# Residual rows turned beside the norm and added on VectorE, in the place of two identity products

## The reference, cut to what matters

```
h = tok(x)                             # patches @ W + b, class token, positions
a = attn(h)                            # sigmoid paths, causal softmax per head, ctx @ Wo
x1 = h + a                             # the first residual: what the change is about
n = layernorm(x1)
f = layernorm(n) * gamma + beta
y = silu(f @ w1 + b1)                  # 256 -> 1024, dequantised weights
out = layernorm(n + 0.5 * (y @ w2 + b2))
```

## Time and profile before

| what | value |
|---|---|
| median of 3 runs | 178.4 us (176.03 to 178.91) |
| the profiled execution | 176.34 us |
| its span, first to last instruction | 174.6 us |
| PE busy | 154.1 us, 88% of the span |
| DVE busy | 94.3 us, 54% |
| POOL busy | 55.6 us, 32% |
| ACT busy | 48.0 us, 27% |
| granted TensorE clock | 0.999 of full |

### The profile page before, as it was taken

The page is one execution under the profiler, slowest core; times in us unless marked ns, Lnnn a source line. Parts: engine busy times, 40 slices in busy tenths (PEclk is TensorE's granted clock), DMA queues, the critical chain, the costliest instruction groups (busy, mean ns, idle before and its releaser), DMA issues.

```text
span 174.6 us, 2987 instructions
## 1 busy us (share of the span) xinstructions
PE 154.1 (88%) x1141; PEld 122.0 (70%) x1141; DVE 94.3 (54%) x175; ACT 48.0 (27%) x105; POOL 55.6 (32%) x129
## 2 busy tenths in 40 slices
PE   0289999799989999899999999999879969979980
PEld 0177878577667797487887778887658858868760
DVE  0065047557777956728647587647547443634232
ACT  0412112523243335114235324226022311032100
POOL 5009811032082603427107218106334022530011
PEclk9999999999999999999999999999999999999999
DMA  5999999700000000000100010000010000000000
GB/s 141 241 241 248 232 369 375 280 2 4 0 2 6 2 0 4 0 0 8 34 0 0 0 34 0 30 4 0 0 32 4 30 0 0 30 34 0 0 30 30
DMA packets 5501, 10.67 MB, mean 61 GB/s; under 512 B 715, under 2 KB 4400, under 8 KB 5232
## 3 DMA queue, kind: packets, MB, share of 16 engines
q1 hardware_dynamic: 5248, 10.30, 20.1%
q10 hardware_dynamic: 240, 0.19, 0.5%
HBM read 9.27 MB, written 1.21 MB: 60 GB/s over the span
## 4 chain that ended last, share of the span: by engine, by line
PE 83%; DVE 6%; DMA 4%; ACT 2%; POOL 2%; issue 1%; ACTq 1%; POOLq 0%
PE bank_z L555 20%; PE bank_s L542 18%; PE bank_z L436 7%; DMA vec_rows<-in_L_ffn_ln_beta 4%; PE bank_s L412 4%; PE bank_p L451 4%; PE bank_s L479 3%; PE bank_p L452 3%; PE bank_s L537 2%; PE bank_w L493 2%; PE bank_p L427 2%; PE bank_o L508 2%; PE bank_o L509 2%; PE bank_z L427 2%; PE bank_o L517 2%; PE bank_w L497 2%
## 5 line engine op out<-in xcount | busy, mean ns | idle before, releaser
L555 PE MATMUL bank_z<-w,act 128*128 128x256 f32 (+1 forms) x160 | 37.0, 381 | 1.8 <-DVE res L830 1.8
L542 PE MATMUL bank_s<-hnT,w 128*128 128x256 f32 (+1 forms) x160 | 35.2, 362 | 0.0
L555 PEld LDWEIGHTS bank_z<-w,act 128*128 128x128 f32 (+1 forms) x160 | 28.1, 182 | 8.0 <-issue 3.2
L542 PEld LDWEIGHTS bank_s<-hnT,w 128*128 128x128 f32 x160 | 28.9, 190 | 5.0
L821 DVE SCALAR_TENSOR_TENSOR act<-th,bank_s 128x512 f32<-128x512 f32 (+1 forms) x20 | 13.0, 648 | 20.3 <-ACT th L691 20.1
L337 POOL TENSOR_TENSOR rstd<-var,exponents 128x3 f32<-128x3 f32 (+1 forms) x10 | 8.9, 893 | 46.9 <-DVE var L805 46.9
L691 ACT ACTIVATE th<-bank_s 128x512 f32<-128x512 f32 (+1 forms) x20 | 11.3, 565 | 32.4 <-PE bank_s L542 32.4
L792 DVE RECIPROCAL recip<-bank_w 128x222 f32<-128x222 f32 (+1 forms) x11 | 16.4, 1494 | 0.7 <-PE bank_w L497 0.7
L675 ACT ACTIVATE phi_q<-bank_p 128x222 f32<-128x222 f32 (+1 forms) x11 | 3.9, 351 | 32.6 <-PE bank_p L461 32.6
L436 PE MATMUL bank_z<-xT,wT 128*128 128x288 f32 x48 | 12.6, 413 | 0.0
L787 DVE TENSOR_TENSOR probs<-probs,allowed 111x888 f32<-111x888 f32 (+1 forms) x11 | 11.5, 1046 | 1.9 <-ACT probs L685 1.9
(11 more groups left out here) (107 smaller groups left out, 242.0 us busy)
## 6 DMA issues: line engine op xcount, KB each, us to landing
x_rows<-in_x SPq DMA_DIRECT2D x6, 576.0 KB, 13.7
q<-in_L_ffn_fc_q SPq DMA_DIRECT2D x2, 1024.0 KB, 20.1
s<-in_L_ffn_fc_scales SPq DMA_DIRECT2D x2, 1024.0 KB, 22.1
out<-fin SPq DMA_DIRECT2D x9, 128.0 KB, 1.7
w_rows<-in_L_tok_W SPq DMA_DIRECT2D x3, 256.0 KB, 8.2
wvp<-in_L_attn_Wv SPq DMA_DIRECT2D x1, 256.0 KB, 10.2
wo<-in_L_attn_Wo SPq DMA_DIRECT2D x1, 256.0 KB, 17.1
b<-in_L_ffn_fc_bias ACTq DMA_DIRECT2D x1, 128.0 KB, 9.6
```

The lines of the kernel that those rows point to most:

```text
L542: last = mm(block[:, i], w1[:, e, f * 128:(f + 1) * 128], hnT[p % 2][:, e, 0:n], start=False, stop=(i == 1 and e == E2 - 1))
L555: last = mm(bank_z[0:w, 0:D], act2[:, f, in_pair(b)], w2[:, f, :], start=(f == 0), stop=(f == FB - 1))
```

## The change

The two identity products leave attention_out. In their place turn_residual(b) transposes the two halves of hT of block b into the second 256 columns of bank_o, residual_rows(b) copies these on ACT to h_rows in SBUF, and normalise(b) on DVE first adds h_rows and the product in bank_o into x1 (two buffers) and takes its statistics there; normed(b) reads x1 too. On PE turn_residual(b + 1) stands directly ahead of turn_normed(b) and waits for the same event, n2 of block b; turn_residual(0) stands in iteration 1, ahead of the patch product of that iteration. attention_out(b) now waits for the copied rows too.

```diff
@@ attention_out, PE
                 pe.wait_ge(ctxT_ready, done)
+                pe.wait_ge(hrow_ready, b + 1)
...
-                mm(bank_o[0:w, 0:D], ctxT[:, 1, tokens_of(b)], wo[:, 1, :], start=False, stop=False)
-                mm(bank_o[0:w, 0:128], hT[:, 0, tokens_of(b)], ident[:], start=False, stop=False)
-                mm(bank_o[0:w, 128:D], hT[:, 1, tokens_of(b)], ident[:], start=False, stop=True).then_inc(attn_psum, 1)
+                mm(bank_o[0:w, 0:D], ctxT[:, 1, tokens_of(b)], wo[:, 1, :], start=False, stop=True).then_inc(attn_psum, 1)
+
+            def turn_residual(b):
+                w = width(b)
+                if b > 0:
+                    pe.wait_ge(n2_ready, b)
+                for e in range(E2):
+                    last = pe.transpose(bank_o[0:w, D + e * 128:D + (e + 1) * 128], hT[:, e, tokens_of(b)], ident[:])
+                last.then_inc(hrow_psum, 1)
@@ the loop, PE
                 if a in TURN_AT:
+                    turn_residual(TURN_AT[a] + 1)
                     turn_normed(TURN_AT[a])
...
                 if a == 1:
+                    turn_residual(0)
                     pe.wait_ge(hT_ready, 2 * E2 + 1)
                     project(2, 1)
...
             weigh(TILES - 1)
+            turn_residual(OUTS - 1)
             turn_normed(OUTS - 2)
@@ ACT
+            def residual_rows(b):
+                w = width(b)
+                act.wait_ge(hrow_psum, b + 1)
+                if b > 0:
+                    act.wait_ge(x1_ready, b)
+                act.activation(h_rows[0:w, :], bank_o[0:w, D:2 * D], ACT.Copy).then_inc(hrow_ready, 1)
...
                 if a in TURN_AT:
                     normed_columns(TURN_AT[a])
+                    residual_rows(TURN_AT[a] + 1)
@@ DVE
             def normalise(b):
                 w = width(b)
                 dve.wait_ge(attn_psum, b + 1)
-                dve.bn_stats(stats[0:w, :], bank_o[0:w, 0:D]).then_inc(stats_ready, 1)
+                dve.wait_ge(hrow_ready, b + 1)
+                tt(x1[b % 2][0:w, :], h_rows[0:w, :], bank_o[0:w, 0:D], ALU.add).then_inc(x1_ready, 1)
+                dve.wait_ge(x1_ready, b + 1)
+                dve.bn_stats(stats[0:w, :], x1[b % 2][0:w, :]).then_inc(stats_ready, 1)
...
-                ts(n2[b % 2][0:w, :], bank_o[0:w, 0:D], mv[0:w, 0:1], rstd3[0:w, 1:2], ALU.subtract, ALU.mult).then_inc(n2_ready, 1)
+                ts(n2[b % 2][0:w, :], x1[b % 2][0:w, :], mv[0:w, 0:1], rstd3[0:w, 1:2], ALU.subtract, ALU.mult).then_inc(n2_ready, 1)
```

More of the change, by code:

```diff
@@ L150, in vit_block @@
         n2 = [sb(f"n2_{i}", [128, D]) for i in range(2)]
+        h_rows = sb("h_rows", [128, D])
+        x1 = [sb(f"x1_{i}", [128, D]) for i in range(2)]
         carry = [sb(f"carry{i}", [128, D]) for i in range(4)]
@@ L198, in vit_block @@
         recip_ready, ctxT_ready = sem("recip_ready"), sem("ctxT_ready")
+        hrow_psum, hrow_ready, x1_ready = sem("hrow_psum"), sem("hrow_ready"), sem("x1_ready")
         attn_psum, stats_ready, mv_ready, var3_ready = sem("attn_psum"), sem("stats_ready"), sem("mv_ready"), sem("var3_ready")
@@ L718, in _ @@
                     x_columns(C + 2)
+                if a == 1:
+                    residual_rows(0)
                 if a in TURN_AT:
                     normed_columns(TURN_AT[a])
+                    residual_rows(TURN_AT[a] + 1)
                 if a in HIDDEN_AT:
@@ L723, in _ @@
                         tanh_of(HIDDEN_AT[a], j)
-            for b in (OUTS - 2, OUTS - 1):
-                normed_columns(b)
+            normed_columns(OUTS - 2)
+            residual_rows(OUTS - 1)
+            normed_columns(OUTS - 1)
             for j in range(4):
```

## The result

The changed kernel takes 180.47 us (median of 4 runs, 180.32 to 181.04) against 177.48 us before (median of 4, 176.03 to 178.91). The ratio is 1.023, with a 95% interval from 1.0186 to 1.0273. The changed kernel is slower; whether by more than 2% the interval leaves open. The predicted time was 180.8 us, the predicted ratio 1.014; the interval lies above that.

The account below looks back on a forecast made before the run. The norm's DVE strand, on or near the path at nine of ten blocks, was taken as the bound, not PE. 9c + 10t - 2.9 gave +2.4 us, 1.4% more, 180.8 us on the median; range 177.4 to 183.0.

Parts of the forecast that it names:

- The strand of the norm: DVE and POOL work (statistics, power, norm) beside PE up to L517; on the path or 0.25 us off at nine blocks.
- c: Growth of the DVE strand per block: add 0.46 less 0.13 saved by the norm from SBUF, 0.33 us; counted at nine blocks.
- t: Pair of residual transposes on PE directly ahead of L517, behind the wait for n: 0.23 us, counted ten times.
- the cover of ACT's copy: PE's other work between L517 and the next product, 3.4 us at shortest, hiding ACT's copy, costed at nothing.
- PE's gain of 0.44: Two residual products (L510, L511) removed from PE ahead of each block's statistics: 0.44 us less per block.
- The second and third rivals: Second: norm gains nothing from SBUF, +3.6 us, chance 0.14. Third: residual pair costs 0.44 us, +4.5 us, chance 0.06.
- The first rival: PE is the bound and the longer DVE strand hides: -2.1 us, 176.3 us; chance 0.12.

Follow-up runs that it names:

- the one with the copy instead: Kernel before, both identity products kept, plus a DVE copy of the product from PSUM to x1, read by statistics and norm: 180.31 us, 1.0251 of before.
- the moved line: Half of block 6's second feed-forward product moved ahead of block 8's transposes: 175.01 us in before, 177.76 in changed, 175.46 in changed with wait for x1.

## Why the prediction was right, and where it was not

The strand of the norm, not PE, sets when the transposes start at eight of the nine blocks behind which a residual is turned: shown. There they start 0.05 to 0.06 us after the norm ends, as in block 2 (70.66 and 70.72) and block 3 (81.25 and 81.31). Block 5 is the exception: there the norm ends at 108.00 and PE comes last, at 108.35. Block by block, from the starts of the work behind the turned norm in the chain of both profiled executions, each less its first patch product:

| block | forecast, us | measured, us |
|---|---|---|
| 0 | +0.79 | +0.81 |
| 1 | +0.56 | +0.82 |
| 2 | +0.06 | -0.07 |
| 3 | 0.00 | +0.01 |
| 4 | +0.35 | +0.27 |
| 5 | +0.03 | +0.18 |
| 6 | +0.38 | +0.30 |
| 7 | +0.12 | +0.09 |
| 8 | +0.56 | +0.66, of it 0.15 by the clock |
| 9 | -0.44 | +1.04, of it 1.52 by the clock |
| sum | +2.4 | +4.1, without the clock +2.4 |

**The terms.** The norm from SBUF costs 0.412 us against the 0.410 taken over from L845; from add to statistics it is 0.44 to 0.46 (144.49 to 144.93) against 0.46; the second pair of transposes adds 0.22 to 0.24 against 0.23; PE has no wait for ACT's rows. c and t hold. One reading in the prediction was off: the row at 52.97 in the earlier trace rows that ends the cover of ACT's copy is DVE's; PE's next product (L508) starts at 52.77, so the shortest cover is 3.25 us and not 3.4. Nothing hung on it.

**Where single blocks were off.** In blocks 4, 6 and 8 I started the add when the silu's record ends; it starts 0.61 us after the silu's start (143.88 to 144.49), 0.08 us before that end. Independence from the silu does not explain it: before, the statistics did not depend on it either and started 0.68 us after its start (90.44 to 91.12). In block 5 I let PE's gain of 0.44 run on to the turned norm, but PE then reached turn_phi 0.20 us too early for phi: a wait that the chain before did not show, because PE came later. In block 1 DVE stood still for 0.32 us between mean and variance:

```profile
56.84 0.22 DVE L832 SCALAR_TENSOR_TENSOR var<-var_scale,mv,var_shift 128x3 f32<-128x3 f32 x1 [0.32 <-DVE mv L828]
```

This gap stands at the same instruction in all five profiles of kernels with the add, and not in the one with the copy instead. Its cause is open. That these errors cancel in the sum is luck.

**What failed.** The term that is missing is the clock. The prediction raised PE's wait at block 8 from 1.87 to 2.4 us ("where PE waited 1.87 us already: c + t") and costed everything behind it at the durations of the trace before. Those were durations at a clock of 1.00. In the changed kernel's trace the clock behind that wait fell to 0.50, for 1.67 us, and all four of its executions have a mean of 0.988 to 0.990. The Trainium skill ("TensorE: Matmul & The Clock Gate", section "HAM oscillation") tells of such a fall: a burst of products starts at half clock when PE has waited between bursts. The trace agrees (0.50 behind waits of 2.19, 2.52 and 2.55 us here), and the recorded clocks show too that the same kernel need not do so in every execution. So the fall is not a price of the change alone: before pays it in ten of 18 executions, and its profiled execution, on whose rows the prediction rests, was one that did not.

**Why the time came out close all the same.** This was luck. 180.8 us was built as a ratio of 1.014 on a median of 178.4, and that is a time of the executions of before whose clock fell (177.68 to 180.02 us); the others lie at 174.93 to 177.10. So the forecast most likely had the clock's price in its base without knowing it, though the clocks of those three executions are not on record. The ratio of 1.023 sets the changed kernel's four executions, all with a fallen clock, against about 176.4 us (180.47 / 1.023), a time of executions of before whose clock held. So it holds the strand and the clock, and the forecast's +1.4%, the strand alone, was short of it. Among executions with a fallen clock the change costs 180.47 - 178.49 = 2.0 us, or 1.1% (178.49 is the median of the ten of before, which ran beside the experiments and not beside the changed kernel), and that is near the forecast. The second and third rivals, the only ones beyond 2%, would have given such a time by another mechanism (a dear norm, dear transposes); both are refuted by the durations above. The first rival, PE as the bound, fell most clearly: PE has 20 instructions less and the end came later.

## What to carry to other kernels

An engine that is 88% busy is not the bound where it waits: compare, place by place, when the two strands that meet there arrive, and count an edit only with what it does to the later one. Where PE waits ahead of dense work, price that work at the lower clock too, and compare executions of equal granted clock before a difference is put down to the change; a few products that are due anyway, moved into the wait, shorten the wait and held the clock in all 18 executions of the moved line here. When an instruction stands behind a wait that it does not need (here the turned residual behind the norm), give it its own wait: that one line was worth 1.8 us at an equal clock, and 3.5 us of the changed kernel's 4.2 with the clock that then held.

## What the hardware showed unexpectedly

In the traces the granted clock fell to 0.50 behind waits of 2.19 to 2.55 us and stayed there for some 3.4 us (over 5 us in one trace) of dense products; behind 1.87 and 1.88 us it was 1.00 (before, and the residual turned inside the wait). No length of wait that decides is shown: ten of 18 executions of before have the low mean all the same. Executions of one kernel differ in it by 2.4 us in the median (178.49 against 176.06 us): idle work in one wait cut the spread from 4.6 to 0.9 us. A 128x256 tensor-scalar operation with two scalar columns takes 544 ns from PSUM and 412 from SBUF, while a copy from PSUM of the same size takes 424 and an add with one PSUM operand 414. So among these rows it is this form from PSUM, not every read of PSUM, that is dear.
